# Routed tokens turned by the DMA transpose as 16-bit halves, in place of TensorE transposes

## The reference, cut to what matters

```python
x = x + gnn(layernorm(x), adj, ...)          # attention over the adjacency, 8 heads of 32
flat = layernorm(x).reshape(8192, 256)
w, idx = top_k(softmax(flat @ router_w), 2); w = w / sum(w)
out = sum over the two experts e of a token: w * (silu(flat @ Wg[e]) * (flat @ Wu[e])) @ Wd[e]
out = out + (silu(flat @ Sg) * (flat @ Su)) @ Sd
x = x + out
```

## Time and profile before

| | |
|---|---|
| median of three runs | 1777.68 us |
| span of the profiled execution, first to last instruction | 1775.1 us |
| TensorE busy | 1711.7 us (96%) |
| VectorE busy | 1280.5 us (72%) |
| ScalarE busy | 1100.3 us (62%) |
| POOL busy | 646.7 us (36%) |
| mean granted TensorE clock | 0.991 of full speed |
| DMA, all queues | 269.19 MB, mean 152 GB/s |

### The profile page before, as it was taken

How to read it: one execution, slowest core, us unless ns; L and a number is a source line. 1 busy time by engine, 2 the same in 40 slices (tenths; PEclk the granted TensorE clock), 3 DMA queues, 4 the chain that set the end, 5 groups by cost and what they waited for, 6 DMA issues and landing times. The chain is left out here.

```text
span 1775.1 us, 35893 instructions
## 1 busy us (share of the span) xinstructions
PE 1711.7 (96%) x12469; PEld 1450.1 (82%) x12469; DVE 1280.5 (72%) x3185; ACT 1100.3 (62%) x2509; POOL 646.7 (36%) x479
## 2 busy tenths in 40 slices
PE   5899999999999999999999999999999999999996
PEld 4678878777878777777788888889898989888986
DVE  4677877877788778777555654777777777777773
ACT  3998888998988889897534333344434443434342
POOL 0135444444554444454121000033343434333343
PEclk8999999999999999998999999999999999999999
DMA  5455566656555655553334265445555555565553
GB/s 147 136 144 144 167 174 174 174 159 179 144 161 174 167 167 169 167 166 120 123 104 143 72 203 177 157 134 159 167 158 151 159 164 160 148 161 164 161 131 36
DMA packets 140946, 269.19 MB, mean 152 GB/s; under 512 B 15072, under 2 KB 92256, under 8 KB 135776
## 3 DMA queue, kind: packets, MB, share of 16 engines
q1 hardware_dynamic: 113760, 230.45, 42.3%
q0 software_dynamic: 26592, 35.67, 9.9%
q10 hardware_dynamic: 416, 0.79, 0.2%
HBM read 141.99 MB, written 74.52 MB: 122 GB/s over the span
## 5 line engine op out<-in xcount | busy, mean ns | idle before, releaser
L871 DVE CUSTOM_DVE_ANT_0 pf<-bank,bias_q 128x512 f32<-128x512 f32 x512 | 350.0, 688 | 167.2 <-PE bank L515 160.5
L1224 POOL DMA_INDIRECT out_x<-yb,ix x142 | 246.8, 1738 | 559.3 <-ACT yb L1447 452.6
L1459 ACT ACTIVATE ah<-am 128x512 fp32r<-128x512 f32 (+1 forms) x220 | 133.1, 605 | 425.6 <-DVE am L1527 425.6
L644 ACT ACTIVATE pf<-pf,nmax 128x512 f32<-128x512 f32 x512 | 375.5, 733 | 28.3 <-DVE nmax L871 28.1
L1358 PE MATMUL bank<-xh,wh 128*128 128x512 f32 (+1 forms) x880 | 334.8, 380 | 0.9 <-ACT pt L632 0.9
L1359 PE MATMUL bank<-xl,wh 128*128 128x512 f32 (+1 forms) x880 | 334.4, 380 | 0.0
L1360 PE MATMUL bank<-xh,wl 128*128 128x512 f32 (+1 forms) x880 | 334.1, 380 | 0.0
L525 PE MATMUL bank<-ident,pf 128*128 128x128 f32 x2048 | 312.3, 275 | 18.7 <-ACT pt L632 18.4
L632 ACT ACTIVATE pt<-bank 128x512 f32<-128x512 f32 x512 | 308.8, 603 | 10.7 <-PE bank L525 9.1
L525 PEld LDWEIGHTS bank<-ident,pf 128*128 128x128 f32 x2048 | 252.0, 141 | 75.7 <-issue 25.6
L1530 DVE TENSOR_TENSOR al<-am,ah 128x512 fp32r<-128x512 f32 (+1 forms) x220 | 146.8, 667 | 147.7 <-ACT ah L1459 147.7
(11 more groups left out here) (209 smaller groups left out, 3073.0 us busy)
## 6 DMA issues: line engine op xcount, KB each, us to landing
raw<-in_w_all SPq DMA_DIRECT2D x39, 1536.0 KB, 7.2
stack<-qk SPq DMA_DIRECT2D x378, 128.0 KB, 2.4
xb<-xg_dram SPq DMA_DIRECT2D x32, 520.0 KB, 7.9
adj_i<-in_adj SPq DMA_DIRECT2D x32, 512.0 KB, 4.3
xn<-in_x SPq DMA_DIRECT2D x16, 512.0 KB, 6.4
xn_dram<-xn SPq DMA_DIRECT2D x16, 512.0 KB
xp<-in_x SPq DMA_DIRECT2D x16, 512.0 KB, 6.6
xnp<-xn_dram SPq DMA_DIRECT2D x16, 512.0 KB, 7.6
```

The costliest lines, as they stand in the source:

```text
L644: act.activation(pf[i][:, :], pf[i][:, :], ACT.Exp, bias=nmax[:, i:i + 1], scale=-1.0, accum_out=den[:, g, tq, j:j + 1]).then_inc(p_exp, 1)
L871: dve.tensor_tensor_reduce(pf[r][:, :], S[p % 2][:, :], bias_q[1 - par][:, tq, :], -SCALE, -3.0 * MASKED, ALU.add, ALU.min, nmax[:, r:r + ...
L1224: pool.indirect_dma_start(out=out, out_offset=bass.IndirectOffsetOnAxis(ap=ix[n % RING][:, i:i + 1], axis=0), in_=yb[s][:, i, :], in_offse ...
L1459: act.activation(ah[s][:, m, 0:cols], am[m % 2][:, 0:cols], ACT.Copy).then_inc(s_ah, 1)
```

## The change

The four extra columns move from `xn2` to a new integer tile `xs` of the same row length (260 words). After normalising, POOL copies `xn2` into `xs` in two copies of 16-bit words: first all upper halves of the 256 features, then all lower halves. The scatter sends `xs`. A routed block's rows are loaded by a DMA transpose (`dma_start_transpose`) of their 512 half-words into `xt16` (128 partitions x 4 x 512), and a second, plain DMA brings the four extra columns into `xm` (16 bytes from each row). ScalarE's new `words(n + 1)` joins the halves with two activations into `xb`, which now holds the turned tokens, as in shared blocks; `high` and `low_x` read `xb`. TensorE's `turn` is gone. `take` reads `xm`. In POOL's slot 25 the wait for the old scatter moves behind the normalising, ahead of the two copies.

```diff
             def scatter(A, j):
                 if j == 0:
                     pool.wait_ge(s_rt, A * RT + RT_IDX)
                     pool.nop().then_inc(s_held_pool, 1)
+                    pool.wait_ge(s_halves, A * 2 + 2)
...
-                    in_=xn2[:, i, :], in_offset=None).then_inc(s_scat, 16)
+                    in_=xs[:, i, :], in_offset=None).then_inc(s_scat, 16)
...
                 if post and p == POOL_AT["xn2"]:
                     pool.wait_ge(s_rstd2, A + 1)
+                    if A > 0:
+                        pool.wait_ge(g_full, unit(b - 1, "X1") + 1)
+                        pool.nop().then_inc(s_held_pool, 1)
+                        pool.wait_ge(s_halves, A * 2)
+                    for i in range(NT):
+                        pool.tensor_scalar(xn2[:, i, :], x1[:, i, :], mv2[:, i, 0:1], rstd2[:, i:i + 1],
+                                           ALU.subtract, ALU.mult).then_inc(s_xn2, 1)
                     pool.wait_ge(s_scat, A * 16 * 2 * NT)
                     pool.nop().then_inc(s_held_pool, 1)
-                    for i in range(NT):
-                        pool.tensor_scalar(xn2[:, i, 0:D], x1[:, i, :], mv2[:, i, 0:1], rstd2[:, i:i + 1],
-                                           ALU.subtract, ALU.mult).then_inc(s_xn2, 1)
+                    pool.wait_ge(s_xn2, A * NT + NT)
+                    for h in range(2):
+                        pool.tensor_copy(xs_half[:, :, D * h:D * h + D], xn2_half[:, :, :, 1 - h]).then_inc(s_halves, 1)
...
-                sp.dma_start(xb[s][:, 0:tl, :], xg_dram[bass.ds(row, P * tl)].rearrange("(p i) d -> p i d", i=tl)
-                             ).then_inc(s_xb[s], 16)
+                tokens = xg_dram[bass.ds(row, P * tl)]
+                sp.dma_start_transpose(xt16[s][:, :, 0:P * tl], tokens.bitcast(U16)[:, 0:2 * D]).then_inc(s_xt[s], 16)
+                sp.dma_start(xm[s][:, 0:tl, :], f32(tokens)[:, D:XW].rearrange("(i p) c -> p i c", p=P)
+                             ).then_inc(s_xm[s], 16)
...
-                if n <= SH:
-                    sp.wait_ge(x_lo, n * KF)
-                else:
-                    sp.wait_ge(x_full, (n - SH) * KF)
+                if n > SH:
+                    sp.wait_ge(s_word, (n - SH) * 2)
                     sp.wait_ge(s_tk, (n - SH) * TK)
...
                 if q == 1:
-                    if after is False:
-                        turn(n + 1, 1 - s)
                     if before is not None:
                         down(n - 1, 1 - s, before)
...
+            def words(n, s):
+                tl = P * tiles(n)
+                act.wait_ge(s_xt[s], (n - SH - s) * 8 + 16)
+                act.wait_ge(x_lo, (n - 1) * KF)
+                halves = flat(s).bitcast(U16).rearrange("p (k t h) -> p k t h", k=KF, h=2)
+                for h in range(2):
+                    act.activation(halves[:, :, 0:tl, 1 - h], xt16[s][:, KF * h:KF * h + KF, 0:tl],
+                                   ACT.Copy).then_inc(s_word, 1)
+
             def high(n, s, shared):
                 if shared:
                     act.wait_ge(s_xb[s], (n - s) * 8 + 16)
-                    if not isinstance(n, int) or n >= 2:
-                        act.wait_ge(u_full, (n - 1) * MT)
+                else:
+                    act.wait_ge(s_word, (n - SH) * 2 + 2)
+                if n >= 2:
+                    act.wait_ge(u_full, (n - 1) * MT)
+                cols = P * tiles(n)
                 for k in range(KF):
-                    if not shared:
-                        act.wait_ge(x_full, (n - SH) * 2 + k + 1)
-                    cols = P * tiles(n)
                     act.activation(xh[s][:, k, 0:cols],
-                                   flat(s)[:, BLOCK * k:BLOCK * k + BLOCK] if shared else TB[k][:, 0:cols],
+                                   flat(s)[:, BLOCK * k:BLOCK * k + cols],
                                    ACT.Copy).then_inc(x_hi, 1)
...
                 silu(n, s, q)
                 if q == 1:
+                    if after is False:
+                        words(n + 1, 1 - s)
                     if after is not None:
                         high(n + 1, 1 - s, after)
```

More of the change, by code:

```diff
@@ L12 @@
 U32 = mybir.dt.uint32
+U16 = mybir.dt.uint16
 ALU = mybir.AluOpType
@@ L69, in attention_phase @@
 def attention_phase(nc, sems, held, banks, x, adj, wqkv, wgate, bg, router_w, xn_dram, x1_dram, xt2_dram, xg_dram,
-                    ident, msum, xn2, idx, s_scat, region):
+                    ident, msum, xn2, xs, idx, s_scat, region):
     NB, N, D = x.shape
@@ L139, in attention_phase @@
         x1 = sb("x1", [P, NT, D])
-        W0, W1, WE, WT = D, D + 1, D + 2, D + 3
+        xs_meta = f32(xs[:, :, D:XW])
         wg_h = sb("wg_h", [P, 2 * KF, D], F32R)
@@ L217, in attention_phase @@
         s_pick = sem("s_pick")
+        s_halves = sem("s_halves")
         s_held_pe, s_held_dve, s_held_pool, s_held_sp = (sem(f"s_held_{e}") for e in ("pe", "dve", "pool", "sp"))
@@ L301, in pieces @@
             return PIECES[p]
-        def f32(t):
-            return t.bitcast(F32)
         def first(b):
@@ L681, in prepare @@
                 dve.wait_ge(s_const, 9)
-                dve.tensor_scalar(xn2[:, :, WT], tok_i[:, :], -float(N), None, ALU.add).then_inc(s_rt0, 1)
+                dve.tensor_scalar(xs_meta[:, :, 3], tok_i[:, :], -float(N), None, ALU.add).then_inc(s_rt0, 1)
                 dve.tensor_copy(iota_e[:, :], iota_i[:, :]).then_inc(s_rt0, 1)
@@ L827, in weigh @@
                 rt = A * RT
-                wv = xn2[:, :, W0:W1 + 1]
+                wv = xs_meta[:, :, 0:2]
                 dve.wait_ge(s_el, A + 1)
@@ L834, in weigh @@
                 dve.wait_ge(s_rt, rt + RT_W0)
-                dve.tensor_copy(xn2[:, :, WE], ef[:, :, 0]).then_inc(s_rt, 1)
-                dve.tensor_scalar(xn2[:, :, WT], xn2[:, :, WT], float(N), None, ALU.add).then_inc(s_rt, 1)
+                dve.tensor_copy(xs_meta[:, :, 2], ef[:, :, 0]).then_inc(s_rt, 1)
+                dve.tensor_scalar(xs_meta[:, :, 3], xs_meta[:, :, 3], float(N), None, ALU.add).then_inc(s_rt, 1)
                 dve.tensor_tensor(wv[:, :, 1], el[:, :], wv[:, :, 0], ALU.mult).then_inc(s_rt, 1)
@@ L951, in pool @@
             pool.wait_ge(s_half, 1)
+            xs_half = xs[:, :, :].bitcast(U16)
+            xn2_half = xn2[:, :, :].bitcast(U16).rearrange("p i (d h) -> p i d h", h=2)
             def scatter(A, j):
@@ L1056, in ffn_phase @@
     assert sum(is_half(r) for r in range(NR)) == NHALF
-    W0, W1, WE, WT = D, D + 1, D + 2, D + 3
+    W0, W1, WE, WT = range(4)
     UNUSED = experts * region
@@ L1138, in ffn_phase @@
         ix = [sb(f"ix{i}", [P, NT], U32) for i in range(RING)]
+        xt16 = [sb(f"xt16_{s}", [P, 2 * KF, BLOCK], U16) for s in range(2)]
+        xm = [sb(f"xm{s}", [P, NT, XW - D]) for s in range(2)]
         raw0 = sb("raw0", [P, WC])
@@ L1153, in ffn_phase @@
         s_xb = [sem(f"s_xb{s}") for s in range(2)]
+        s_xt = [sem(f"s_xt{s}") for s in range(2)]
+        s_xm = [sem(f"s_xm{s}") for s in range(2)]
+        s_word = sem("s_word")
         s_x1b = [sem(f"s_x1b{s}") for s in range(2)]
@@ L1159, in ffn_phase @@
         s_tk = sem("s_tk")
-        x_full = sem("x_full")
         x_hi = sem("x_hi")
@@ L1320, in body @@
                                  pad[:, :, 0:D]).then_inc(s_pad, 16)
-                    sp.dma_start(xg_dram[UNUSED:UNUSED + BLOCK].rearrange("(q p) d -> p q d", p=P),
+                    sp.dma_start(f32(xg_dram[UNUSED:UNUSED + BLOCK]).rearrange("(q p) d -> p q d", p=P),
                                  pad[:, :, :]).then_inc(s_pad, 16)
@@ L1326, in body @@
                         row = sp.value_load(ends[0:1, e:e + 1], min_val=0, max_val=(experts - 1) * region + TOKENS)
-                        sp.dma_start(xg_dram[bass.ds(row, BLOCK)].rearrange("(p q) d -> p q d", q=NT),
+                        sp.dma_start(f32(xg_dram[bass.ds(row, BLOCK)]).rearrange("(p q) d -> p q d", q=NT),
                                      pad[:, :, :]).then_inc(s_tail, 16)
@@ L1344, in tensor @@
         def tensor(pe):
[L1345 to L1354, removed]
             def split(out_, lh, ll, rh, rl, first, last):
@@ L1425, in high @@
                     act.wait_ge(s_xb[s], (n - s) * 8 + 16)
[L1426 to L1433 removed]
+                else:
[3 more added lines that the diff above has]
+                cols = P * tiles(n)
+                for k in range(KF):
+                    act.activation(xh[s][:, k, 0:cols], flat(s)[:, BLOCK * k:BLOCK * k + cols],
                                    ACT.Copy).then_inc(x_hi, 1)
@@ L1511, in low_routed, with low_x @@
                 low(s, part, parts(n, False))
-            def low_x(n, s, shared):
+            def low_x(n, s):
                 for k in range(KF):
@@ L1516, in low_x @@
                     cols = P * tiles(n)
-                    dve.tensor_tensor(xl[s][:, k, 0:cols], flat(s)[:, BLOCK * k:BLOCK * k + BLOCK] if shared else
```

(23 more changed lines are left out.)

## The result

The changed kernel takes 1815.34 us (median of four runs, 1814.6 to 1816.6) against 1777.28 us for the kernel before on the same chip: a ratio of 1.022, with a 95% interval of 1.0207 to 1.0232. It is 38 us slower, in the direction that was forecast and with more than twice the forecast's +17 us. The profiled execution has a span of 1814.9 us, 39.8 us above that of before.

The account below looks back on a forecast made before the run. TensorE bounds the experts, with VectorE's loop with ScalarE hardly shorter; 66 us of join waits make that loop 12 or 21 us longer than TensorE's time, middle +17 us on 1777.7: 1795 us, own range 1784 to 1815, whole range 1758 to 1832.

Parts of the forecast that it names:

- 1.18 us per block: Routed experts: VectorE's spare time, its waits for TensorE, 34.1 us in 29 blocks; anything beyond makes its loop the longer.
- The prediction's full loop: VectorE's timeline in a full block: weight splits, products, `xl` and `take` sum to 15.5 us; joins add 1.95 us.
- two readings: VectorE's loop with 66 us added: by waits 21 us later than TensorE ends now, by the block's timeline 12 us.
- the one open thing: ScalarE's joins: a 16-bit join assumed to cost as a copy of as many 32-bit elements; forecast chance 0.55.
- the prediction's own factor: ScalarE's joins in the experts: a change per join is multiplied by 2 x 34.5 full-block joins.
- the upper bound: ScalarE's joins: at twice the time, from strided 2-byte stores, they would add 72 us: 1867 us.
- TensorE's 30 us: Experts: chain slots of the removed transposes over 38 steps, the whole gain if nothing else bound the experts.
- the low end: DMA transpose per full block: 1.5 us, as the plain load; extra columns 0 of 0 to 3.1 us.
- the 9.8 us from which they were to decide: DMA-bound rival, chance 0.20: transpose and extra columns decide above 9.8 us of all engines per full block; high end 1991 us.
- The first rival: TensorE stays the bound, kernel faster: joins under 0.80 us; 1765 us, or 1748 with joins hidden altogether; chance 0.20.
- Costed at nothing: POOL's two copies per batch (2.4 us taken), moved scatter wait, SyncE's two DMA issues, among others: no added time.
- One named sign of being wrong: Experts: a granted clock below 1.00 behind TensorE's gaps would show the forecast wrong.

## Why the prediction was right or wrong

**What bounds the experts** was right: a second loop, VectorE with ScalarE's answers, that is hardly shorter than TensorE's and that two joins make the longer one. The place where it would show (`xl` waiting for `xh`) is the place where it shows. But 1.18 us per block is a mean of unlike steps: up to 2.0 us in a full step of the kernel before, none in two of the three around each half block. The prediction's full loop with joins of 1.05 us, 15.5 + 1.95 = 17.45 us, is below TensorE's 17.7; the run with packed stores has steps of 17.4 us and, around a half block, 14.6, 16.1 and 17.4. So with joins as priced the whole loss lies around the half blocks. That the sum still came out right is in part luck: it is the middle of two readings, 12 and 21 us, neither of which saw this.

**The size was off in one term.** The step that failed is "the one open thing is that a 16-bit join costs as a copy of as many 32-bit elements". The row taken, 1.049 us, copies into adjacent words; the join stores every other 16-bit word, and takes 1.350. By the prediction's own factor that is 0.30 us x 69 joins = 21 us, and 17 + 21 = 38 us, the measured difference; 66 + 21 = 87 us is the measured wait. The run with packed stores gives the forecast back: joins of 1.041 us, 66.9 us of waits where 66 were added up, 1796 us where 1795 was forecast. A smaller misreading: 1.049 and 0.616 us are not quite one rate per element, since the second 512 elements add 0.43 us and the first take 0.62; the half joins were priced by their own row, so the sum does not suffer. I had named strided stores as the upper bound, at twice the time, but set the forecast's own range by joins of at most 1.2 us; it ended at 1815 us, and the measured 1815.34 lies just past that edge.

**TensorE's 30 us** were right as a price, 28 us when put back where TensorE is the bound, and right to be left out of the sum here: put back into the changed kernel they cost nothing.

**The DMA transpose** was costed at the low end and hidden, and it is hidden. Its engine time was not at the low end. By the shares of the hardware queue, transpose and extra columns take 0.476 x 1814.9 - 0.423 x 1775.1 = 113 us more than the load before (that queue's share was 42.3% then), 3.2 us per full block; with 1.5 us for that load some 4.7 us (an estimate), about half of the 9.8 us from which they were to decide. The Trainium skill's sentence that such transposes are as fast as regular DMAs (Advanced Engine Details and Errata, X-Bar Transpose (TRN2)) does not quite hold here: the hardware queue's share is 47.6% with the transpose and 42.7% with the plain load, and the load lands after 10.7 us instead of 9.3. The Trainium skill's rule against it (DMA: Bandwidth & Descriptors, first table: below 512 B a transfer misses line rate) points the way that the trace shows, with 107200 packets under 512 B in the one and 33872 in the other, but the time does not hang on it.

**The first rival**, faster with TensorE as the bound, needed joins of under 0.80 us; they are 1.35. The run with the joins in quarter 0 shows its end state, 1751 us, close to the 1748 us for joins hidden altogether.

**Costed at nothing** was right: POOL's copies (1.03 us each, below the 2.4 that I took as the nearest row), the moved scatter wait, SyncE's longer issue. The attention's TensorE time is the same to the hundredth. One named sign of being wrong did show, a granted clock below 1.00 (0.99) behind TensorE's gaps; with the packed stores its mean is 0.989, nearly as low as the changed kernel's 0.988, at 19 us less.

## What to carry to other kernels

Work that was put on an idle engine cost nothing here only where nobody stood in order behind it: ScalarE was busy for 41% of the experts, and 2.7 us per block in the wrong place cost 64 us more than in the right one. Before adding a step, read the waits of the engine that waits for it, sum the spare time of that whole loop, for each kind of block by itself and not as a mean, and look for the stretch in which the helper itself sits waiting. And price a copy by a row with the same strides, not only the same number of elements.

## What was not expected of the hardware

A ScalarE copy that stores every other 16-bit word takes 1.350 us for 1024 elements where a packed store takes 1.041 (0.770 and 0.615 for 512).

A VectorE instruction whose operands all lie in SBUF was held while POOL's 16-bit copies ran: one cast of 1024 columns took 3.43 us beside 3.21 us of POOL copies, and 0.69 us ahead of them; over the kernel that is 90 us of VectorE. The one time that `am`, which reads PSUM, ran beside a copy from start to end (1590.91 us), it took its usual 0.68 us. POOL's pair of copies took 2.61 us the one time that VectorE ran only a PSUM operation beside them (1101.17 us), where a pair takes 3.2 us beside the operations in SBUF and took 2.0 in the attention, with packed stores. So POOL's copies grow too, but only part of the step from 2.0 to 3.2 us is VectorE's doing. The Trainium skill states such sharing (GPSIMD Engine Reference, Key points: POOL shares its SBUF interfaces with VectorE, with contention for instructions in a 2-port mode or with two SBUF inputs). The trace agrees for `wl` and `al`, which have two SBUF inputs (`wl` 4.45 us, `al` 3.25, where 1.23 and 0.69 are usual); the cast has one, and no run here shows its mode.

A DMA transpose of 0.5 MB held its issuing queue for a median of 6.6 us, where a plain load's issue took 0.34 us, and 0.56 in the run that puts one in its place.
